# A graph network kernel on one core: the high and low parts of the last 53 node rows share one product

## What is computed

```python
n_nodes = node_feats.shape[0]                      # 3125
for _ in range(6):
    h = jnp.maximum(node_feats @ W1.T + b1, 0.0) @ W2.T + b2
    msg = jax.ops.segment_sum(h[src], dst, num_segments=n_nodes)
    gx = msg @ W_ih.T + b_ih
    gh = node_feats @ W_hh.T + b_hh
    xr, xz, xn = jnp.split(gx, 3, axis=-1)
    hr, hz, hn = jnp.split(gh, 3, axis=-1)
    r = jax.nn.sigmoid(xr + hr)
    z = jax.nn.sigmoid(xz + hz)
    n = jnp.tanh(xn + r * hn)
    node_feats = (1.0 - z) * n + z * node_feats
```

## Time and profile before

| what | us |
|---|---|
| median of 3 executions | 2048.14 (2046.22 to 2049.36) |
| the profiled execution | 2045.75 |
| its span, first to last instruction | 2043.7 |
| TensorE busy | 1864.3 (91%) |
| VectorE busy | 1104.2 (54%) |
| ScalarE busy | 575.3 (28%) |
| GpSimd busy | 335.9 (16%) |

### The profile page before, as it was taken

How to read it: one execution, slowest core, us unless ns; L and a number is a source line. 1 busy time by engine, 2 the same in 40 slices (tenths; PEclk the granted TensorE clock), 3 DMA queues, 4 the chain that set the end, 5 groups by cost and what they waited for, 6 DMA issues and landing times.

```text
span 2043.7 us, 30436 instructions
## 1 busy us (share of the span) xinstructions
PE 1864.3 (91%) x10923; PEld 1118.3 (55%) x10924; DVE 1104.2 (54%) x2615; ACT 575.3 (28%) x1183; POOL 335.9 (16%) x454
## 2 busy tenths in 40 slices
PE   2769999999799999999999999999999999929996
PEld 2645555555344574445744457444574455629996
DVE  6867888864144652444524445234452456635775
ACT  0234444432021231122311223112231112216663
POOL 1011111100355500000000000000000013143665
PEclk7789999999899999999999999999999999959998
DMA  8930000000443300000000000000000001463543
GB/s 261 336 131 1 1 1 1 1 1 1 138 140 134 129 22 2 1 1 1 1 2 1 1 1 1 2 1 1 1 1 1 11 32 60 182 263 66 84 77 53
DMA packets 73943, 109.43 MB, mean 54 GB/s; under 512 B 11774, under 2 KB 64809, under 8 KB 72516
## 3 DMA queue, kind: packets, MB, share of 16 engines
q1 hardware_dynamic: 50526, 49.36, 7.7%
q0 software_dynamic: 18368, 38.09, 7.4%
q10 hardware_dynamic: 4902, 20.01, 2.4%
HBM read 43.59 MB, written 65.05 MB: 53 GB/s over the span
## 4 chain that ended last, share of the span: by engine, by line
PE 69%; issue 14%; POOL 6%; DVE 6%; ACT 2%; DMA 1%; POOLq 0%; SPq 0%; ACTq 0%; DVEq 0%
PE bank L1514 35%; PE bank L1538 24%; PE bank L1551 4%; PE bank L1491 4%; POOL out L584 3%; POOL slot_in L561 2%; POOL tick L583 1%; PE bank L1402 1%; DMA x_kept<-x_lo 1%; PE bank L1486 1%; DVE hot_key L852 1%; ACT stage L1204 1%; DVE r_lo L767 1%; DVE xa L723 0%; ACT m_hi L1177 0%
## 5 line engine op out<-in xcount | busy, mean ns | idle before, releaser
L1514 PE MATMUL bank<-adj,r_hi 128*128 128x512 fp8e4 (+4 forms) x2100 | 732.0, 352 | 0.0
L1514 PE MATMUL bank<-adj,r_lo 128*128 128x512 fp8e4 (+4 forms) x2100 | 732.0, 352 | 0.0
L1514 PEld LDWEIGHTS bank<-adj,r_hi 128*128 128x128 f16 x2100 | 205.7, 98 | 188.1 <-issue 1.4
L1514 PEld LDWEIGHTS bank<-adj,r_lo 128*128 128x128 f16 x2100 | 205.6, 98 | 188.1 <-issue 1.3
L774 DVE SCALAR_TENSOR_TENSOR m_lo<-bank,msg_unit,m_hi 128x512 f16<-128x512 f32 (+4 forms) x84 | 57.2, 682 | 280.9 <-ACT m_hi L1177 280.9
L1538 PE MATMUL bank<-x_hi,wht_hi 128*128 128x512 f16 (+4 forms) x504 | 177.4, 352 | 0.8 <-DVE m_lo L774 0.5
L1538 PE MATMUL bank<-m_hi,wct_hi 128*128 128x512 f16 (+4 forms) x504 | 177.3, 352 | 0.0
L1538 PE MATMUL bank<-m_lo,wct_hi 128*128 128x512 f16 (+4 forms) x504 | 177.3, 352 | 0.0
L1538 PE MATMUL bank<-m_hi,wct_lo 128*128 128x512 f16 (+4 forms) x504 | 177.3, 352 | 0.0
L1538 PE MATMUL bank<-x_lo,wht_hi 128*128 128x512 f16 (+4 forms) x504 | 177.3, 352 | 0.0
L1538 PE MATMUL bank<-x_hi,wht_lo 128*128 128x512 f16 (+4 forms) x504 | 177.3, 352 | 0.0
(11 more groups left out here) (288 smaller groups left out, 2918.5 us busy)
## 6 DMA issues: line engine op xcount, KB each, us to landing
slot_in<-fill_rows SPq DMA_DIRECT2D x2, 13520.0 KB, 68.7
ffn_scratch<-pair POOLq DMA_DIRECT2D x32, 512.0 KB, 3.2
ffn_w<-ffn_scratch ACTq DMA_DIRECT2D x8, 2048.0 KB, 16.1
x_rows<-in_L_ffn_W POOLq DMA_DIRECT2D x32, 256.0 KB, 3.9
slot_x<-slot_in SPq DMA_DIRECT2D x30, 260.0 KB, 3.3
xa<-in_x SPq DMA_DIRECT2D x1, 3072.0 KB
x<-in_x ACTq DMA_DIRECT2D x1, 3072.0 KB
out<-x SPq DMA_DIRECT2D x4, 512.0 KB
```

The costliest lines, as they stand in the source:

```text
L1514: last = mm(bank[f][:, 0:n], r[:, q, f * P:(f + 1) * P], c, start=q == 0 and i == 0, stop=q == NT - 1 and i == len(todo) - 1)
```

## The change

Rows 0 to 63 of tile 24 are written a second time into rows 64 to 127, in `adj` (by a transfer of 64 rows for each window of step 0, from SP's queue), and in the columns of the state (`x_hi` and `x_lo` get columns 3136 on as a copy of columns 3072 on). The relu of tile 24 thus comes out twice, in rows 0 to 63 and in rows 64 to 127. In rows 64 to 127 of `r_hi` VectorE then puts the low part, so that `r_hi` of tile 24 holds high parts above and low parts below, and one product with the doubled rows of `adj` sums both. The second product of tile 24 (`r_lo`) is left out in all windows, halves and steps.

```diff
--- before.py
+++ after.py
@@ -67,6 +67,9 @@
 FUSED_A = sum(FUSED_WIN[u] < NW - 3 for u in range(USES))
 FUSED_B = sum(FUSED_WIN[u] < NW - 1 for u in range(USES))
 RELU_BUILD = 9
+TWIN = P // 2
+TWIN_COL = (NT - 1) * P
+assert TAIL <= TWIN
 CHUNK_Q = (0, 4, 8, 12, 16, 19, 22, NT)
 GATE_OPS = 9
 XS = 16.0
@@ -406,6 +410,10 @@
             sp.dma_start(bound_dram.rearrange("(t p) b -> p t b", p=P), bound[:]).then_inc(sem("bound_out"), 16)
             sp.wait_ge(sem("bound_out"), 16)
             sp.dma_start(bound_row[:], bound_dram.rearrange("(a p) b -> a (p b)", a=1)).then_inc(sem("bound_in"), 16)
+            for w in range(TURNS):
+                c0, c1 = w * TURN_COLS, (w + 1) * TURN_COLS
+                sp.wait_ge(sem("stage_free"), GROUP // 2 * (w + 1))
+                sp.dma_start(adj[TWIN:P, NT - 1, c0:c1], adj[0:TWIN, NT - 1, c0:c1]).then_inc(sem("adj_twin"), 16)
             slow = read_slow_flag(sp)
             with sp.If(slow > 0):
                 with sp.Fori(0, NSL) as sl:
@@ -715,7 +725,12 @@
                 dve.wait_ge(sem("xt_hi"), u + 1)
                 ins = v.tensor_tensor(x_lo[:, :, 2 * P * u:2 * P * u + m],
                                       bank[2 + u % 2][:, 0:DT * m].rearrange("p (t n) -> p t n", t=DT),
-                                      x_hi[:, :, 2 * P * u:2 * P * u + m], ALU.subtract)
+                                      x_hi[:, :, 2 * P * u:2 * P * u + m], ALU.subtract) if u < USES - 1 else None
+                for h in range(2 if u == USES - 1 else 0):
+                    c0 = TWIN_COL + h * TWIN
+                    ins = v.tensor_tensor(x_lo[:, :, c0:c0 + TWIN],
+                                          bank[2 + u % 2][:, 0:DT * m].rearrange("p (t n) -> p t n", t=DT)[:, :, 0:TWIN],
+                                          x_hi[:, :, c0:c0 + TWIN], ALU.subtract)
                 ins.then_inc(*((sem("xt_lo"), 1) if u < USES - 1 else (sem("state_lo"), NW)))
 
             dve.wait_ge(sem("rstd_ready"), 1)
@@ -764,6 +779,11 @@
 
                 m = min(2, NT - 2 * u)
                 dve.wait_ge(sem(again + "relu_hi"), g + 1)
+                if u == USES - 1:
+                    twin = r_hi[TWIN:P, NT - 1, :]
+                    v.scalar_tensor_tensor(twin, bank[4 + u % 4 if first else 2 + u % 2][TWIN:P, 0:D], 0.0, twin, ALU.max, ALU.subtract)\
+                     .then_inc(sem(again + "relu_lo"), 1)
+                    return
                 v.scalar_tensor_tensor(r_lo[:, 2 * u:2 * u + m, :].rearrange("p t d -> p (t d)"), bank[4 + u % 4 if first else 2 + u % 2][:, 0:m * D], 0.0,
                                        r_hi[:, 2 * u:2 * u + m, :].rearrange("p t d -> p (t d)"), ALU.max, ALU.subtract)\
                  .then_inc(sem(again + "relu_lo"), 1)
@@ -823,8 +843,12 @@
             def state_lo(s, w, again=""):
                 n, c0 = columns_of(s, w, again)
                 dve.wait_ge(sem(again + "state_hi"), NW * s + w + 1)
-                v.tensor_tensor(x_lo[:, :, c0:c0 + n], x_new[:, :, 0:n], x_hi[:, :, c0:c0 + n], ALU.subtract)\
-                 .then_inc(sem(again + "state_lo"), 1)
+                ins = v.tensor_tensor(x_lo[:, :, c0:c0 + n], x_new[:, :, 0:n], x_hi[:, :, c0:c0 + n], ALU.subtract)
+                if w == NW - 1:
+                    m = c0 + n - TWIN_COL
+                    ins = v.tensor_tensor(x_lo[:, :, TWIN_COL + TWIN:TWIN_COL + TWIN + m], x_new[:, :, n - m:n],
+                                          x_hi[:, :, TWIN_COL + TWIN:TWIN_COL + TWIN + m], ALU.subtract)
+                ins.then_inc(sem(again + "state_lo"), 1)
 
             def hots(g):
                 i, b = divmod(g, GROUP)
@@ -1147,8 +1171,12 @@
             def state_part(u):
                 m = min(2, NT - 2 * u) * P
                 act.wait_ge(sem("xt"), u + 1)
-                a.activation(x_hi[:, :, 2 * P * u:2 * P * u + m], bank[2 + u % 2][:, 0:DT * m].rearrange("p (t n) -> p t n", t=DT),
-                             ACT.Copy).then_inc(sem("xt_hi"), 1)
+                xt = bank[2 + u % 2][:, 0:DT * m].rearrange("p (t n) -> p t n", t=DT)
+                if u < USES - 1:
+                    a.activation(x_hi[:, :, 2 * P * u:2 * P * u + m], xt, ACT.Copy).then_inc(sem("xt_hi"), 1)
+                else:
+                    a.activation(x_hi[:, :, TWIN_COL:TWIN_COL + TWIN], xt[:, :, 0:TWIN], ACT.Copy)
+                    a.activation(x_hi[:, :, TWIN_COL + TWIN:NPAD], xt[:, :, 0:TWIN], ACT.Copy).then_inc(sem("xt_hi"), 1)
 
             act.wait_ge(sem("w_tr"), 1)
             a.activation(w1t[0][:], bank[4][:].rearrange("p (t j) -> p t j", t=DT), ACT.Copy).then_inc(sem("w_hi"), 1)
@@ -1194,7 +1222,11 @@
             def state_hi(s, w, again=""):
                 n, c0 = columns_of(s, w, again)
                 act.wait_ge(sem(again + "gate_ops"), half(s, w, 2) * GATE_OPS + LEAD)
-                a.activation(x_hi[:, :, c0:c0 + n], x_new[:, :, 0:n], ACT.Copy).then_inc(sem(again + "state_hi"), 1)
+                ins = a.activation(x_hi[:, :, c0:c0 + n], x_new[:, :, 0:n], ACT.Copy)
+                if w == NW - 1:
+                    m = c0 + n - TWIN_COL
+                    ins = a.activation(x_hi[:, :, TWIN_COL + TWIN:TWIN_COL + TWIN + m], x_new[:, :, n - m:n], ACT.Copy)
+                ins.then_inc(sem(again + "state_hi"), 1)
 
             def evict(g):
                 i, b = divmod(g, GROUP)
@@ -1506,10 +1538,12 @@
                     pe.wait_ge(sem(again + "msg_lo"), half(s, 0, 0) + 1)
                     mm(bank[0][:, 0:2], ones_h[:], b1_rows[:, 0:2], start=True, stop=True)
                 if exact:
-                    pe.wait_ge(sem("planes_in"), (s + 1) * (32 * NW) + 32 * (w + 1))
+                    pe.wait_ge(sem("planes_in"), (s + 1) * (PLANES * NW) + PLANES * (w + 1))
                 for q in range(q0, q1):
+                    if fused and q == NT - 1:
+                        pe.wait_ge(sem("adj_twin"), 16 * (w + 1))
                     counts = [planes[:, i, q, 0:n] for i in range(2)] if exact else [adj[:, q, c0:c0 + n]]
-                    todo = [(r, c) for c in counts for r in (r_hi, r_lo)]
+                    todo = [(r, c) for c in counts for r in ((r_hi, r_lo) if q < NT - 1 else (r_hi,))]
                     for i, (r, c) in enumerate(todo):
                         last = mm(bank[f][:, 0:n], r[:, q, f * P:(f + 1) * P], c,
                                   start=q == 0 and i == 0, stop=q == NT - 1 and i == len(todo) - 1)
```

More of the change, by code:

```diff
@@ L334, in gnn_ffn @@
         EXACT_STORED = 32 * NSL + 1
+        PLANES = 2 * 3 * 16
         def read_slow_flag(engine):
@@ L421, in load_planes @@
                     for i in range(2):
-                        sp.dma_start(planes[:, i, :, 0:n], plane_dram[i][:, :, c0:c0 + n]).then_inc(sem("planes_in"), 16)
+                        sp.dma_start(planes[:, i, 0:NT - 1, 0:n], plane_dram[i][:, 0:NT - 1, c0:c0 + n]).then_inc(sem("planes_in"), 16)
+                        for p0 in (0, TWIN):
+                            sp.dma_start(planes[p0:p0 + TWIN, i, NT - 1, 0:n], plane_dram[i][0:TWIN, NT - 1, c0:c0 + n]).then_inc(sem("planes_in"), 16)
                 for w in range(NW):
@@ L1614, in _ @@
                 for w in range(NW):
-                    pe.wait_ge(sem("planes_in"), 32 * (w + 1))
+                    pe.wait_ge(sem("planes_in"), PLANES * (w + 1))
                     if w >= 4:
@@ L1619, in _ @@
                         for i in range(2):
-                            last = mm(bank[4 + w % 4][:, 0:WIN_LEN[w]], ones_h[:], planes[:, i, q, 0:WIN_LEN[w]],
+                            m = P if q < NT - 1 else TWIN
+                            last = mm(bank[4 + w % 4][:, 0:WIN_LEN[w]], ones_h[0:m, :], planes[0:m, i, q, 0:WIN_LEN[w]],
                                       start=q == 0 and i == 0, stop=q == NT - 1 and i == 1)
```

## The result

The changed kernel takes 2032.96 us (median of 4 executions, 2031.04 to 2033.69), the kernel before 2047.93 (4 executions, 2046.22 to 2049.36). The ratio is 0.9926, with an interval of 0.9909 to 0.9943: 0.74% faster. The profiled execution took 2031.04 us, its span is 2029.1. Against the span before, 2043.7, that is 14.6 us less; the forecast had 14.5.

A forecast was written before the change was run, and what follows sets the result against it. TensorE's queue was taken to bound the kernel. 15.84 removed - 0.86 lost - 0.4 - 0.1 added = 14.5 us, so 2048.14 - 14.5 = 2033.6 us, range 2030.5 to 2037.5.

The forecast's parts named there:

- What is removed: One product in 50 per window and half, 84 in all: 13.20 us in steps 1 to 5, 2.64 in step 0.
- Rival B: In step 0's build, VectorE or the eviction sets the pace, eating most of 2.64 us: 2036.2 us; chance 0.07.
- Rival A: A removed product costs less than its spacing, down to its 98 ns weight load: 7.3 us, 2040.8; chance 0.03.
- What of it is lost: Window 0, looped steps: removing half 1's product only lengthens the wait for msg_lo; four steps lose 0.86 us.
- What is added: Costs of the added work: state operations 0.4 us, first state's pieces 0.1, relu_lo of tile 24 and doubling transfers 0.
- The state operations: One more 108-column operation each in state_hi and state_lo, last window: 0.4 us at step 0's end, nothing in steps 1 to 4.
- The doubling transfers: Seven transfers in the build, with 15.6 us of room before tile 24 is wanted: cost 0.
- rival E: Doubling transfers land late and tile 24 waits; the gain is gone from 17.7 us after the copy on; chance 0.02.
- The first state's pieces: Last piece of the first state written in two operations on both engines, ahead of x_kept: at most 0.36 us, taken as 0.1.
- `relu_lo` of tile 24: Now 64 rows of 256 columns in place of 128 rows; the columns set its length, so cost 0.
- Rival C: TensorE's clock falls in window 0's gap, 0.2 us wider, in five steps: 10.2 us come back, 2043.8; chance 0.02.
- Rival D: End of step 5 isn't rigid: chains could start 2.8 us earlier or later, 2030.8 or 2036.4 us; chance 0.08, shared.

The follow-up runs named there:

- the kernel with 128 rows: The changed kernel, but relu_lo of tile 24 works on all 128 rows, still over its own operand in r_hi: 2028.43 us.
- the four kernels: Changed kernel, products put back in step 0 alone: all windows, last window, windows 0 to 5, 14 in window 0: 2034.60, 2027.47, 2034.23, 2034.25 us.

## Why the prediction was right, and where its terms were off

The time came within 0.7 us of 2033.6, and the gain in span within 0.1 us of the 14.5 forecast. The mechanism was right: what is removed costs its spacing, and one wait eats a part of it. But that the sum came so close is luck: two gains that no term had (the clock and the start of the build, 2.0 us) stand against losses that no term had or that were priced at nothing (the relu and the loop's gaps, 1.9 us). By the steps of the prediction:

- **What is removed.** A product costs its spacing. In step 0 the turns gave 2.26 and the last window 0.36 of the 2.64 us expected, a turn going from 48.91 to 48.53 us. Rival B, a build that doesn't follow, is refuted by that. In the loop the pieces of 49 take 10.60 us (10.57 expected), and 14 products put back cost 2.65 (2.639 expected). Rival A falls with it: at the weight load's 98 ns they would have cost 1.4. The Trainium skill, page "TensorE: Matmul & The Clock Gate", section "Back-to-back issue gap", has 131 ns for a product of 512 columns in such a stream; the trace after shows 10.60 / 49 = 0.216 us again, and the measurement decides.
- **What of it is lost.** 0.216 us in each looped step, by the wait for `msg_lo` that grew from 0.27 to 0.49. Right, and shown by the product put back there at no cost. In step 5 both products counted, as argued; but there `m_lo` starts 0.79 us after the transposition in the chain and not 0.67.
- **What is added.** The state operations cost 0.37 us (0.4 taken) and nothing in the loop. The doubling transfers cost nothing: they land in 1.8 us, where 15.6 us are free, and rival E is out. The first state's pieces, taken as 0.1 us, can't be read: the build began 0.81 us earlier in this profile, which is within what it varies by (123.3 to 125.0 us in all).
- **The term that was mis-sized** is `relu_lo` of tile 24, "so 0". The operation did keep its length, but it no longer begins before the one ahead of it ends. It costs 0.13 us in each of steps 1 to 5, 0.65 in all, shown by the timeline and the kernel with 128 rows. The 0.12 us of step 5 between the transposition and `m_lo` belong to it too: with 128 rows `m_lo` starts 0.67 us after the transposition again. Together that is 0.77 us where the sum had nothing.
- **What no term had.** The clock at the end of step 0: 1.55 us gained, in these two profiles; the four kernels show that it hangs on when the gap ends. Rival C looked for a fall of the clock in a gap of window 0; none came there, and the one that mattered was already in the kernel before. Then 1.12 us lost at the entry into the loop (0.44), at three starts of a loop round (0.54 in all) and in the first 88 products (0.14). The gaps at the loop's rounds are 1.05 to 1.68 us long in the 14 profiles without an order that follows an edit; they are scatter.
- **The rest** took 278.23 and 278.33 us. Rival D, that the end isn't rigid, holds for other runs: in four profiles ScalarE reads the last sums 0.33 us after their product's start and not 1.6 to 3.2 us, and the whole end varies by 4.7 us. Here it came out even.

The looped step checks the parts: -2.639 + 0.216 + 0.13 = -2.29 us. Step 4 gave -2.30. Steps 1, 2 and 3 gave -1.81, -2.16 and -2.22, which is the same with the loop's gaps (and in step 1 the 0.14) taken off. Step 5: -2.64 + 0.13 for the relu and some 0.12 in the chain from the transposition to `m_lo`, -2.39; it gave -2.38. All in all 14.5 was 15.8 - 1.3 on paper, and in the trace it was 15.8 removed, 1.6 from the clock, 0.5 from an earlier start of the build, less 0.9 of `msg_lo`, 0.4 of the state, 0.65 of the relu, 0.1 behind the transposition, 1.1 of the loop's gaps and 0.1 at the end: 14.6.

## What to carry to other kernels

Where one engine fills its queue, a removed instruction is worth its spacing of starts, and the first thing to look for is a wait right behind it that eats it; the same wait tells where instructions can be moved to for nothing, which was worth nearly as much here (0.9926 - 0.9871 of 2048 us, 11 us beyond the change) as the change itself. An operation cut down to part of the partitions isn't free because its length stays: look at when it starts. And when a forecast hits, check its terms all the same: one piece that runs at half clock in only one of two profiles can hide several small errors.

## What the runs showed of the hardware that was not expected

- An idle time of TensorE of 2.35 us at the end of step 0 was followed by a fall to the low clock when it ended at 499.3 us of this program or later (at once in three profiles, some 0.5 to 1 us after in the other three), and by the full clock when it ended at 498.4 or earlier, in 14 of 14 profiles.
- A VectorE operation on rows 64 to 127 starts behind the end of the operation on 128 rows ahead of it (0.72 us after its start); on 128 rows it starts 0.61 us after it, 0.08 before its end. In step 5 a copy that follows some 3 us later also starts 0.11 us later when that operation has 64 rows.
- A transfer of 28 KB from one part of SBUF to another landed in 1.8 us.
